# Recurrent stage: two kinds of elementwise work move from GpSimd to VectorE

## What is computed

```python
x = layernorm(rows + experts_out)              # end of layer 0
xn = ln(x, ln1_g, ln1_b)
xp = shift(xn)                                 # the row of the token before
k = (xn * mix_k + xp * (1 - mix_k)) @ Wk       # v and r likewise
wkv = scan over time of exp(k) * v and exp(k)  # a / (b + eps)
x = x + (sigmoid(r) * wkv) @ Wo
yn = ln(x, ln2_g, ln2_b)
yp = shift(yn)
kk = square(relu((0.5 * yn + 0.5 * yp) @ Wfk))
rr = sigmoid(yn @ Wfr)
x = layernorm(x + x_in + rr * (kk @ Wfv))
```

## Time and profile before

| | us |
|---|---|
| median of the runs | 2408.03 |
| the profiled execution's own time | 2405.2 |
| its span in the trace | 2403.5 |
| recurrent pipeline, from the first gather (1213.0) to the last root (1544.0) | about 331 |

### The profile page before, as it was taken

How to read it: one execution, slowest core, us unless ns; L and a number is a source line. 1 busy time by engine, 2 the same in 40 slices (tenths; PEclk the granted TensorE clock), 3 DMA queues, 4 the chain that set the end, 5 groups by cost and what they waited for, 6 DMA issues and landing times. The chain is left out here.

```text
span 2403.5 us, 53002 instructions
## 1 busy us (share of the span) xinstructions
PE 1930.3 (80%) x16756; PEld 1583.7 (66%) x16788; DVE 1573.7 (65%) x6410; ACT 1303.5 (54%) x3105; POOL 1042.7 (43%) x1282
## 2 busy tenths in 40 slices
PE   7788888888888789999948988578988884997720
PEld 6455555555555588898837777468888874986610
DVE  2388888888888658442248999477788748433355
ACT  3588888888888442344427888534444420563310
POOL 1233333333333131656568887422222210777765
PEclk9699999999999799999969999889999955997755
DMA  6798999899888410555621222200000020664433
GB/s 225 244 308 302 295 298 303 294 297 304 295 297 294 139 53 1 162 165 174 169 56 39 60 60 56 49 1 1 1 1 1 1 105 4 199 200 138 130 91 78
DMA packets 198095, 353.98 MB, mean 147 GB/s; under 512 B 25280, under 2 KB 145856, under 8 KB 196800
## 3 DMA queue, kind: packets, MB, share of 16 engines
q1 hardware_dynamic: 140752, 294.77, 37.8%
q0 software_dynamic: 17664, 36.21, 6.3%
q10 hardware_dynamic: 39408, 19.60, 2.8%
HBM read 165.87 MB, written 145.52 MB: 130 GB/s over the span
## 5 line engine op out<-in xcount | busy, mean ns | idle before, releaser
L670 POOL TENSOR_SCALAR_AFFINE_SELECT attend_raw_relative<-attend_raw_relative 128x508 f32<-128x508 f32 x256 | 161.3, 654 | 530.6 <-ACT attend_raw_relative L506 530.6
L1357 POOL DMA_INDIRECT moe_route_rows_sb<-tokens,moe_taken x296 | 281.3, 950 | 195.9 <-PE moe_route_bank L1397 80.0
L426 PE MATMUL attend_turn_bank<-ident,attend_score 128*128 128x128 f32 x1536 | 241.9, 284 | 70.4 <-DVE attend_heads L591 50.0
L1515 DVE COPY moe_route_y<-moe_route_bank 128x128 f32<-128x128 f32 x296 | 86.0, 291 | 307.8 <-PE moe_route_bank L1416 300.5
L506 ACT COPY attend_raw_relative<-attend_rel_bank 128x768 f32<-128x768 f32 x256 | 205.0, 801 | 114.4 <-PE attend_rel_bank L399 106.8
L426 PEld LDWEIGHTS attend_turn_bank<-ident,attend_score 128*128 128x128 f32 x1536 | 166.5, 141 | 151.5 <-DVE attend_heads L591 65.1
L1456 ACT COPY moe_route_rows_t<-moe_route_bank 128x128 f32<-128x128 f32 x296 | 78.5, 265 | 321.3 <-PE moe_route_bank L1397 319.9
L512 ACT ACTIVATE attend_prob_t<-attend_turn_bank 128x384 f32<-128x384 f32 x512 | 229.1, 488 | 34.7 <-PE attend_turn_bank L426 34.6
L570 DVE CUSTOM_DVE_ANT_0 attend_score<-attend_score_bank,attend_relative 128x128 f32<-128x128 f32 x512 | 146.7, 286 | 128.4 <-PE attend_score_bank L399 68.4
L579 DVE TENSOR_SCALAR attend_score<-attend_score,attend_extreme 128x256 f32<-128x256 f32 x512 | 219.1, 428 | 0.0
L1416 PE MATMUL moe_route_bank<-moe_w,moe_route_hid 128*128 x1184 | 215.5, 308 | 3.3 <-DVE moe_route_y L1515 2.1
(11 more groups left out here) (318 smaller groups left out, 5092.4 us busy)
## 6 DMA issues: line engine op xcount, KB each, us to landing
shear<-attend_raw_relative SPq DMA_DIRECT2D x128, 768.0 KB, 5.0
attend_relative<-shear SPq DMA_DIRECT2D x128, 768.0 KB, 6.6
moe_route_w_now<-moe_w SPq DMA_DIRECT2D x296, 129.0 KB
expert_out<-moe_route_y ACTq DMA_DIRECT2D x73, 256.0 KB
qk_heads<-project_qk SPq DMA_DIRECT2D x32, 256.0 KB, 3.0
heads_qk<-qk_heads SPq DMA_DIRECT2D x128, 64.0 KB
tokens<-moe_z SPq DMA_DIRECT2D x8, 1024.0 KB, 3.9
moe_route_rows_sb<-tokens,moe_taken POOLq DMA_INDIRECT x296
```

The lines of the kernel that those rows point to most:

```text
L426: mm = nc.tensor.transpose(bank[:, j * P:(j + 1) * P], score[:, (h - LAG) % RING, j * P:(j + 1) * P], c.ident[:, :])
L670: m = nc.gpsimd.affine_select(out=future, in_=future, compare_op=ALU.is_ge, fill=-BIG, base=1 - P, pattern=[[0, QUAD], [1, P - 1]], channe ...
L1357: nc.gpsimd.indirect_dma_start(rows_sb[:, s % TAKEN, :], None, c.tokens, bass.IndirectOffsetOnAxis(ex.taken[:, s // S, s % S:s % S + 1], 0 ...
```

## The change

`add_old` leaves GpSimd's loop, where it stood between the second and the third gather, and becomes a call in VectorE's loop behind `gate_second(i - 5)` and ahead of `divide(i - 1)`. The two small instructions of `scale` that write `bases` leave GpSimd too; as `shift_variances(i)` they stand in VectorE's loop between `double(i - 5)` and `gate_second(i - 5)`. GpSimd keeps the gathers and the power. The waits move along with the instructions; the semaphore of the constant -1/2 has a name of its own.

```diff
+            def add_old(t):
+                dve.wait_ge(yn_ready, t + 1)
+                wait_past(dve, k_made, 2 * t - 2)
+                nc.vector.tensor_tensor(both[t % 2][:, :], yn[t % 2][:, 1:], yn[t % 2][:, 0:T], ALU.add).then_inc(both_ready, 1)
+
+            def shift_variances(turn):
+                u = turn % 2
+                dve.wait_ge(moments_done, moments_made(turn))
+                wait_past(dve, rooted, scales_made(turn - 2))
+                nc.vector.tensor_scalar(bases[u][:, 0:3, :], moments[u][:, :, :, 1], 1.0, LN_EPS, ALU.mult, ALU.add)
+                nc.vector.tensor_scalar(bases[u][:, 3:5, :], moments[u][:, 0::2, :, 1], 1.0 + LN_EPS, LN_EPS ** 2, ALU.mult, ALU.add
+                                        ).then_inc(based, 1)
...
                 if live(i - 5):
                     double(i - 5)
+                if i in scaled:
+                    shift_variances(i)
+                if live(i - 5):
                     gate_second(i - 5)
+                if live(i - 3):
+                    add_old(i - 3)
                 if live(i - 1):
                     divide(i - 1)
...
             def scale(i):
                 u = i % 2
-                pool.wait_ge(moments_done, moments_made(i))
+                pool.wait_ge(halved, 1)
+                pool.wait_ge(based, scales_made(i))
...
-                nc.gpsimd.tensor_scalar(bases[u][:, 0:3, :], moments[u][:, :, :, 1], 1.0, LN_EPS, ALU.mult, ALU.add).then_inc(based, 1)
-                nc.gpsimd.tensor_scalar(bases[u][:, 3:5, :], moments[u][:, 0::2, :, 1], 1.0 + LN_EPS, LN_EPS ** 2, ALU.mult, ALU.add
-                                        ).then_inc(based, 1)
-                pool.wait_ge(based, 2 * scales_made(i) + 1)
                 nc.gpsimd.tensor_tensor(roots[u][:, :, :], bases[u][:, :, :], minus_half[:, :, :], ALU.pow).then_inc(rooted, 1)
 
-            def add_old(t):
-                pool.wait_ge(yn_ready, t + 1)
-                wait_past(pool, k_made, 2 * t - 2)
-                nc.gpsimd.tensor_tensor(both[t % 2][:, :], yn[t % 2][:, 1:], yn[t % 2][:, 0:T], ALU.add).then_inc(both_ready, 1)
-
-            nc.gpsimd.memset(minus_half[:, :, :], -0.5).then_inc(based, 1)
+            nc.gpsimd.memset(minus_half[:, :, :], -0.5).then_inc(halved, 1)
             for i in turns:
                 ahead = i + LEAD
                 if live(ahead):
                     gather(ahead, 0)
                     gather(ahead, 1)
-                if live(i - 3):
-                    add_old(i - 3)
                 if live(ahead):
                     gather(ahead, 2)
```

More of the change, by code:

```diff
@@ L1653, in recur @@
         stats_done = [sem(f"stats_done{k}") for k in range(3)]
-        half_summed, summed, row_ready, moments_done, based, rooted, shifted, ratio2_done, rest_done = (
-            sem(x) for x in ("half_summed", "summed", "row_ready", "moments_done", "based", "rooted", "shifted", "ratio2_done", "rest_done"))
+        half_summed, summed, row_ready, moments_done, based, halved, rooted, shifted, ratio2_done, rest_done = (
+            sem(x) for x in ("half_summed", "summed", "row_ready", "moments_done", "based", "halved", "rooted", "shifted", "ratio2_done", "rest_done"))
         gathered = c.indirect["moe0_gathered"]
```

## The result

The changed kernel takes 2500.1 us (median of six runs, 2496.9 to 2505.7) against 2408.7 us before (2406.8 to 2410.8): ratio 1.0376, 95% interval 1.0362 to 1.0389, or 91.4 us more. 2495 was forecast. The profiled execution took 2502.5 us, with a span of 2500.5 us.

The account below looks back on a forecast made before the run. No engine was full; a circle of waits through `shift`, aggregates and power set the 8.95 us turn. New circle +62 and clock falls +25 made +87 us: 2492 on the profiled execution, 2495 us on the median scale; range 2460 to 2520.

Parts of the forecast that it names:

- old circle: Recurrent pipeline: `shift` through aggregates on VectorE, then GpSimd's power, back to `shift`; 8.95 us, the turn before the change.
- the other path: `keys` and `project` on TensorE, exponents on ScalarE, then `weigh`; nearly as tight, with 0.19 us of slack before `weigh`.
- The variances: Two small instructions moved to VectorE: 0.2 us of its order (0.15 to 0.35), power starting 0.2 us earlier.
- The add: `add_old` moved from GpSimd to VectorE: GpSimd loses 0.62 us a turn; on VectorE the add takes 0.41 us.
- new circle: Late add, `keys`, `project`, exponents, `weigh`, `gate_second`, back to the add: 11.2 us a turn, 2.27 above 8.95.
- the large part: Turns 5 to 31 on the new circle: 27 turns at 2.27 us more each, 61 us.
- The small parts: Turns 4 and 32 add 1 us each; the last turns give back 1 to 2 through the earlier power.
- The clock: TensorE's clock falls behind its 2.25 us hole in one of two turns, 1.8 us each: 25 us, bounds 0 and 50.
- A: Rival: TensorE's clock holds and only the new circle counts, 2408 + 62 = 2470 us; chance 0.22.
- B: Rival: TensorE's clock falls in nearly every turn, 2408 + 62 + 50 = 2520 us; chance 0.12.
- C: Rival: faster; slack absorbs the late add, the old circle goes from 8.95 to about 8.7, 2401 us; chance 0.06.
- E: Rival: VectorE's added work slows GpSimd's power by 0.24 us, 9 us if on the path; D or E deciding 0.05.

Follow-up runs that it names:

- var_only: Changed kernel with the add moved back to GpSimd, so only the variances move to VectorE; -5.9 us against the kernel before, ratio 0.9964 to 0.9988.
- order_only: Kernel before with only TensorE's order changed to project, output, keys; -0.6 us against before, ratio 0.9988 to 1.0006.
- var_direct: Add on GpSimd as in `var_only`, but variances on VectorE directly behind the aggregates, ahead of `double`; -11.7 us against the kernel before.
- keys_behind: Changed kernel, add still late, with TensorE's order project, output, keys instead of keys, project, output; -9.3 us against the kernel before.
- fill: Changed kernel plus four unread TensorE matmuls per turn between `receptance` and the next `keys`; +63.8 us against the kernel before.
- add_only: Kernel before with only the add moved to its late place on VectorE, variances left on GpSimd; +81.5 us against before.
- add_mid: Changed kernel with the add between `invert` and the aggregates in VectorE's order; +32.3 us against the kernel before.
- add_early: Changed kernel with the add ahead of `invert` in VectorE's order instead of behind `gate_second`; +1.0 us against the kernel before.
- direct_behind: `var_direct` with TensorE's order project, output, keys; -11.1 us against the kernel before, ratio 0.9940 to 0.9967.

## Why the prediction was right

*What bounded the kernel before.* The old circle, `shift` to aggregates to power to `shift`, holds. `var_only` took 0.12 us out of it and the turn fell by 0.12; `order_only` touched the other path and nothing moved.

*The variances.* I took 0.2 us of VectorE's order and 0.2 us of earlier start. Measured are 0.14 (1340.66 to 1340.80 in the changed kernel) and 0.13: both terms were a little too large. `var_direct`, with a mean turn of 8.72 us against the 8.83 of `var_only`, shows that the place behind `double` gave part of the gain away.

*The add.* 0.42 us against 0.41 taken.

*The new circle.* 11.20 us against 11.2 forecast, and each of its waits is where it was expected: `keys` idle 2.33 us (2.25), `weigh` waits, `shift` no longer. The three places of the add and `keys_behind` show that it is this circle and no other. The circle's share of the loss is 62 us in the forecast and 61.7 us in `fill`'s trace. Nearly all of it is the large part: turns 5 to 31 cost 61.8 us there, 61 in the forecast. The small parts were less exact and cancelled: turns 4 and 32 cost 1.1 us together instead of 2, the turns behind them cost 0.7 us instead of giving back 1 to 2 (in the changed kernel they give back 1.2), and the first four gave back 1.9, which the forecast had left out.

*The clock.* One fall in two turns at 1.8 us was taken, 25 us in all. Measured are 14 in 25 turns at 1.69 us, and 25.8 us in all between first and last power. `fill` shows that the long turns are the falls. That the share came so close is luck: the earlier trace rows show only that the clock falls behind some holes and not behind others (in the trace of the kernel before it is at 1.2 GHz behind 5 of those 14), and one half was a choice. The price was near the truth by another sum: not all of `keys` ran at the lower clock. From the start of `keys` to that of `project` the long turn takes 1.11 us more (2.94 against 1.83), and the start of `project` adds the other 0.58. The Trainium skill (TensorE: Matmul & The Clock Gate, HAM oscillation) tells of a loop whose clock falls at every wait for data, but those waits are longer than the 2.33 us here, and the rule given there allows gaps of this length. The clock fell all the same in 14 of 25 turns, and the measurement decides.

*The rivals.* A (the clock holds) is what `fill` measured, 63.8 us above before, and the changed kernel is not it. B fell with the 11 short turns. C named a real gain, but it comes only where the add holds up nothing: with the variances alone, or with the late add and TensorE's other order. The sharing of E is not seen in the power. Its median is 1.98 us with the variances on VectorE and the add left on GpSimd (`var_only`), and 1.98 with both moved; it is 2.09 with the add alone on VectorE (`add_only`), and 2.09 before. So it goes with the place of the variances, for a reason that stays open, and not with the add. The Trainium skill (GPSIMD Engine Reference, Key points) has GpSimd contend with VectorE's instructions of two SBUF inputs; of the moved add the power's time shows nothing of the kind.

## What to carry to other kernels

In a software pipeline whose engines keep a fixed order, an instruction that moves to another engine takes its place in that engine's queue. Before moving it, follow its result through every queue behind it, and see whether the path comes back to the point at which it was put; if it does, and the circle is longer than the turn was, its length is the new turn, however empty the engines are. In this kernel the earliest place in the order at which the inputs are there cost nothing that could be measured, the late one 91 us, and with `keys` out of the way of `project` the late one did no harm either. And when a circle leaves TensorE idle, look whether the clock stays: work in the hole can shorten the turn.

## What the runs showed of the hardware

- An idle stretch of TensorE of 2.33 us in a turn of 11.2 us, with a second one of 0.84 us before `turn`, was enough to bring its clock from 2.4 to 1.2 GHz in 14 of 25 turns. With 1.3 us (`add_mid`) or 0.6 us (`fill`) in place of the 2.33 it stayed at 2.4 in the middle of the stage. A fall in the middle cost the same 1.69 us each time.
- GpSimd's gathers lasted 0.94 to 0.95 us at the start of the stage (the first nine of the changed kernel). The median of the 128 was 1.05 us before the change, 0.95 to 0.96 in the three kernels whose VectorE waited long (the changed one, `add_only`, `fill`), and 1.01 to 1.02 in `var_only`, `add_early`, `add_mid`, `keys_behind`, `var_direct` and `direct_behind`. It does not simply follow VectorE's busy share: 91% before, 99% in `keys_behind`. What lengthens them is not shown.
- The kernel before took 2530.7 us on one chip and 2409 to 2410 us on two others. The turns of the recurrent stage had the lengths expected from the other chips to 0.1 us; the rest of the program was longer there: the first power came some 30 us later (1263 to 1268 us against 1228 to 1235), and behind the last one 946 to 950 us passed instead of 860 to 863. Why stays open.
